# First layer of a two-layer kernel: weight split in halves, an earlier input split, and two gate products moved to where dummy transposes stood

## The reference

```
x = x + attn0(layernorm(x))      # gated, scanned linear attention, 6 heads of 64
x = x + moe(layernorm(x))        # router over 16 experts (top 2), plus 2 shared experts
x = x + attn1(layernorm(x))      # causal softmax attention, 16 heads of 128
x = x + ffn(layernorm(x))        # 688 wide, weights looked up from a table of 16 values
```

```
state = rotate(state, phi) * sigmoid(alpha) + sigmoid(beta) * rotate(v, psi)
out   = rotate(state, -theta)
y     = (out * rms(out) * rms_w * silu(g)) @ Wo
```

## Time and profile before

| | us |
|---|---|
| median of 3 runs | 2258.48 (2257.07 to 2265.22) |
| the profiled execution, its own time | 2264.6 |
| its span, first to last instruction | 2262.8 |
| first layer up to the expert pass, about | 515 |
| PE busy in the span | 2157.7 (95%) |
| DVE busy | 1678.0 (74%) |
| ACT busy | 1375.8 (61%) |
| POOL busy | 539.8 (24%) |
| mean granted clock of TensorE | 0.979 |

### The profile page before, as it was taken

The page is one execution under the profiler, slowest core; times in us unless marked ns, Lnnn a source line. Parts: engine busy times, 40 slices in busy tenths (PEclk is TensorE's granted clock), DMA queues, the critical chain, the costliest instruction groups (busy, mean ns, idle before and its releaser), DMA issues. The chain is left out here.

```text
span 2262.8 us, 37592 instructions
## 1 busy us (share of the span) xinstructions
PE 2157.7 (95%) x13012; PEld 1869.8 (83%) x13012; DVE 1678.0 (74%) x4385; ACT 1375.8 (61%) x3554; POOL 539.8 (24%) x522
## 2 busy tenths in 40 slices
PE   6899999878998999999999999999999999999995
PEld 5677777746788899889988988998898898899884
DVE  7888897788875777876776776686677678767663
ACT  4543443025646766775786777578667767856861
POOL 0212322420113323222311312222232132122210
PEclk9999999888999999999999999999999999999998
DMA  8001000326641112111211211211121121111100
GB/s 290 1 1 52 24 33 24 129 97 197 177 126 38 61 52 66 57 43 61 71 38 38 89 43 38 80 52 38 61 71 50 40 75 57 38 52 52 40 4 19
DMA packets 88539, 145.81 MB, mean 64 GB/s; under 512 B 8352, under 2 KB 55840, under 8 KB 88352
## 3 DMA queue, kind: packets, MB, share of 16 engines
q1 hardware_dynamic: 67104, 111.94, 15.5%
q0 software_dynamic: 6144, 16.79, 2.1%
q10 hardware_dynamic: 15104, 14.68, 1.9%
HBM read 105.63 MB, written 37.75 MB: 63 GB/s over the span
## 5 line engine op out<-in xcount | busy, mean ns | idle before, releaser
L585 POOL TENSOR_TENSOR wo_low<-wraw_o,wo_high 128x256 fp32r<-128x256 f32 x128 | 94.5, 739 | 1101.3 <-ACT wo_high L630 1101.3
L922 ACT ACTIVATE pr<-bank,negmax 128x128 f32<-128x128 f32 (+3 forms) x512 | 263.1, 527 | 143.5 <-DVE negmax L1447 143.5
L1037 DVE TENSOR_TENSOR p_low<-bank,p_high 128x512 fp32r<-128x512 f32 (+2 forms) x384 | 190.1, 550 | 116.2 <-ACT p_high L630 115.8
L630 ACT ACTIVATE p_high<-bank 128x512 fp32r<-128x512 f32 (+2 forms) x384 | 177.8, 497 | 150.0 <-PE bank L1946 150.0
L1447 DVE CUSTOM_DVE_ANT_0 bank<-bank,causal 128x128 f32<-128x128 f32 (+3 forms) x512 | 234.6, 520 | 1.1 <-PE bank L1602 1.1
L1474 DVE SCALAR_TENSOR_TENSOR xs<-bank,rinv,xs 128x256 f32<-128x256 f32 x512 | 211.6, 474 | 1.2 <-PE bank L1602 1.2
L1600 PE MATMUL bank<-h_high,wqk_high 128*128 128x512 f32 x512 | 203.1, 397 | 2.2 <-DVE h_low L1037 2.2
L1601 PE MATMUL bank<-h_low,wqk_high 128*128 128x512 f32 x512 | 203.1, 397 | 0.0
L1602 PE MATMUL bank<-h_high,wqk_low 128*128 128x512 f32 x512 | 202.7, 396 | 0.0
L575 POOL TENSOR_TENSOR wqk_low<-wraw,wqk_high 128x512 fp32r<-128x512 f32 x128 | 165.6, 1294 | 82.8 <-ACT wqk_high L630 82.8
L1037 DVE TENSOR_TENSOR z_low<-bank,z_high 128x512 fp32r<-128x512 f32 x128 | 88.4, 691 | 129.0 <-ACT z_high L630 128.9
(11 more groups left out here) (312 smaller groups left out, 6457.4 us busy)
## 6 DMA issues: line engine op xcount, KB each, us to landing
wraw<-in_wpair SPq DMA_DIRECT2D x64, 512.0 KB, 4.0
wraw<-in_wpair SPq DMA_DIRECT2D x64, 256.0 KB, 4.4
wraw_o<-in_wpair SPq DMA_DIRECT2D x64, 256.0 KB, 2.5
tokens_by_expert<-zero SPq DMA_DIRECT2D x10, 1024.0 KB, 10.5
xt<-tokens_by_expert SPq DMA_DIRECT2D x40, 256.0 KB, 3.2
expert_results<-ey ACTq DMA_DIRECT2D x40, 256.0 KB, 3.7
wres<-in_wexp SPq DMA_DIRECT2D x1, 6144.0 KB, 20.6
xs<-x_between_stages SPq DMA_DIRECT2D x8, 512.0 KB, 4.5
```

Source lines behind the costliest of these rows:

```text
L585: pool.tensor_tensor(wo2[e][1][:], wraw_o[r][:, e, :], wo2[e][0][:].bitcast(F32), ALU.subtract).then_inc(s_wo, 1)
L630: sc.activation(dst, src, ACT.Copy, scale=scale).then_inc(done, 1)
L922: ins = sc.activation(pr[:, i, 0:(i + 1) * P], score(i), ACT.Exp, scale=-1.0, bias=negmax[:, i:i + 1], accum_out=rsum[:, i:i + 1])
L1037: v.tensor_tensor(at(parts[1]), src, high_, ALU.subtract).then_inc(done, 1)
```

## The change

- ACT runs a one-column Copy into a new tile `warm` before anything else.
- The high part of the weights is made in two instructions instead of one: quantities 0 to 3 as soon as the loads are in, then unit 0's normalisation (unit_apply), then the wait for POOL's copies and quantities 4 to 7. DVE's low part is made in two halves too, with input_low(0) between them. PE waits for the second half before the first gate products.
- ACT does input_high(1) after gates(0, (8, 9)), ahead of sin_cos(0, 2) and gates(0, (10, 11)).
- In the loop the gate products of places 10 and 11 go from behind places 8 and 9 to behind conv_products(y, 2), where the 44 dummy transposes stood, which go away. ACT reads these two products after router_norm(x) and scales them after router_input(x). The second half of the router's transposes waits for that reading. Semaphore counts follow.

```diff
-MIDDLE_TURNS = (12, 44)
+MIDDLE_TURNS = 12
@@ ACT
+            sc.activation(warm[:], ident[:, 0:1], ACT.Copy)
...
-            sc.wait_ge(s_setup, 2)
-            high(w8[0] ... all eight quantities, s_w8h)
-            unit_apply(0, 0, xu[0], xn1, s_xn1, s_ln1)
+            sc.wait_ge(s_const, 16 * CONST_DMAS)
+            high(w8[0][:, :, 0:4, :] ..., s_w8h)
+            unit_apply(0, 0, xu[0], xn1, s_xn1, s_ln1)
+            sc.wait_ge(s_setup, 2)
+            high(w8[0][:, :, 4:8, :] ..., s_w8h)
             input_high(0)
...
             gates(0, (8, 9))
+            input_high(1)
             sin_cos(0, 2)
             gates(0, (10, 11))
-            input_high(1)
...
                 spread_rms(x)
-                gates(y, (10, 11))
                 sin_cos(y, 0)
...
                 router_norm(x)
+                gates_taken(y, (10, 11))
                 router_input(x)
+                gates_scaled(y, (10, 11))
                 sin_cos(y, 2)
@@ DVE
-            v.wait_ge(s_w8h, 1)
-            v.tensor_tensor(w8[1][:], w8raw[:], w8[0][:].bitcast(F32), ALU.subtract).then_inc(s_w8l, 1)
-            input_low(0)
+            for n in range(2):
+                quants = slice(4 * n, 4 * n + 4)
+                v.wait_ge(s_w8h, n + 1)
+                v.tensor_tensor(w8[1][:, :, quants, :], ..., ALU.subtract).then_inc(s_w8l, 1)
+                if n == 0:
+                    input_low(0)
@@ PE, gate_products
-                    if p >= 2:
+                    if p >= 10 and u > 0:
+                        pe.wait_ge(s_res, 2 * u)
+                    elif p >= 2:
                         pe.wait_ge(s_gr, 12 * u + p - 1)
+                    elif u == 1:
+                        pe.wait_ge(s_gr, 12)
@@ PE, loop
             conv_products(0, 0, (2, 3))
+            pe.wait_ge(s_w8l, 2)
             gate_products(0, (0, 1, 2, 3))
...
-                gate_products(y, (8, 9, 10, 11))
+                gate_products(y, (8, 9))
...
                 conv_products(y, 2, (2, 3))
-                pe.wait_ge(s_res, 2 * x + 1)
-                clock_turns(MIDDLE_TURNS[1], 6)
-                router_turn(x)
+                gate_products(y, (10, 11))
+                unit_turn(x, xm, s_xm, (6, 7, 4, 5), s_t2, (0,))
+                pe.wait_ge(s_gr, 12 * y + 12)
+                unit_turn(x, xm, s_xm, (6, 7, 4, 5), s_t2, (1,))
```

More of the change, by code:

```diff
@@ L162, in two_layer_program @@
             half_pi = sa("half_pi", [P, 1])
+            warm = sa("warm", [P, 1])
             headsum = sa("headsum", [P, 4])
@@ L679, in gates, with gates_taken @@
             def gates(u, places):
+                gates_taken(u, places)
+                gates_scaled(u, places)
+            def gates_taken(u, places):
                 for p in places:
@@ L691, in gates, with gates_scaled @@
                         sc.activation(dst, src, ACT.Tanh, scale=0.5).then_inc(s_gr, 1)
+            def gates_scaled(u, places):
                 for p in places:
@@ L749, in shared_silu @@
                 sc.activation(sg2[n % 2][:], bank[shared_bank(u, n)][:], ACT.Silu).then_inc(s_ss, 1)
+            sc.wait_ge(s_const, 16 * CONST_DMAS)
+            high(w8[0][:, :, 0:4, :].rearrange("p k q n -> p k (q n)"),
+                 w8raw[:, :, 0:4, :].rearrange("p k q n -> p k (q n)"), s_w8h)
+            unit_apply(0, 0, xu[0], xn1, s_xn1, s_ln1)
             sc.wait_ge(s_setup, 2)
-            high(w8[0][:].rearrange("p k q n -> p (k q n)"), w8raw[:].rearrange("p k q n -> p (k q n)"), s_w8h)
-            unit_apply(0, 0, xu[0], xn1, s_xn1, s_ln1)
+            high(w8[0][:, :, 4:8, :].rearrange("p k q n -> p k (q n)"),
+                 w8raw[:, :, 4:8, :].rearrange("p k q n -> p k (q n)"), s_w8h)
             input_high(0)
@@ L1286, in _ @@
             v.wait_ge(s_const, 16 * CONST_DMAS)
-            v.wait_ge(s_w8h, 1)
-            v.tensor_tensor(w8[1][:], w8raw[:], w8[0][:].bitcast(F32), ALU.subtract).then_inc(s_w8l, 1)
-            input_low(0)
+            for n in range(2):
+                quants = slice(4 * n, 4 * n + 4)
+                v.wait_ge(s_w8h, n + 1)
+                v.tensor_tensor(w8[1][:, :, quants, :], w8raw[:, :, quants, :], w8[0][:, :, quants, :].bitcast(F32),
+                                ALU.subtract).then_inc(s_w8l, 1)
+                if n == 0:
+                    input_low(0)
             v.wait_ge(s_const2, 16 * CONST2_DMAS)
@@ L1659, in rms_turn @@
                 if r == 2 and u + 1 < NU:
-                    pe.wait_ge(s_gr, 12 * (u + 1) + 11)
+                    pe.wait_ge(s_gr, 12 * (u + 1) + 9)
                 for i in range(NT):
@@ L1669, in out_product @@
                 if ab == 1 and u + 1 < NU:
-                    pe.wait_ge(s_gr, 12 * (u + 1) + 12)
+                    pe.wait_ge(s_gr, 12 * (u + 1) + 10)
                 half = slice(ab * P // 2, (ab + 1) * P // 2)
@@ L1702, in out_product_part @@
                     ins.then_inc(s_o0, 1)
-            def router_turn(u):
-                pe.wait_ge(s_res, 2 * u + 2)
-                unit_turn(u, xm, s_xm, (6, 7, 4, 5), s_t2)
             def router_logits_part(u, ab):
@@ L1795, in _ @@
                 gate_products(y, (4, 5))
-                clock_turns(MIDDLE_TURNS[0], 7)
+                clock_turns(MIDDLE_TURNS, 7)
                 square_sums(x, 1)
```

## The result

The changed kernel takes 2271.06 us (median of 12 runs, 2267.35 to 2276.68) against 2257.43 for the kernel before on the same chip: ratio 1.0061, 95% interval 1.0049 to 1.0072, so 13.6 us slower. The forecast was 2264 us, within 0.5% as the likeliest case and slower by over 0.5% with a chance of 0.20. The time lies in the range of 2249 to 2277; the first comparison lies just on the slow side of 0.5%, the second just within.

What follows compares the result with a forecast made beforehand. PE, busy 95% of the span, was taken as the bound through its waits and half-clock time in the first layer. -8.0 + 4.5 + 9.5 = +6 on the median of 2258.5 gave 2264 us, range 2249 to 2277.

Steps and rivals of the forecast that it cites:

- The start and the first boundary: Start and step from unit 0 to unit 1: rexp of y = 1 earlier, -8.0 us, bounds -5.3 and -10.5.
- the 5 us: Sign at the step from unit 0 to unit 1: the forecast is wrong if that boundary gives less than 5 us.
- The lead of the input itself: Unit 1's input: with input_high(1) first, DVE's low part ends 5.3 us earlier, the start's 0.7 included.
- POOL beside DVE: Unit 1's first rotation: POOL's two beta multiplications slow DVE, cost 1.1 us, at least 0, up to 2.2.
- PE is ahead of DVE there: Unit 1 after the early input: PE has no half clock and no wait of 4.9; gate products 8 and 9 end at 103.5.
- The rms turns: Three loop turns: removing products 10 and 11 gains 0, leaves PE idle 3.1 us; clock falls cost 1.5 each, +4.5 us.
- The router's part: Three turns: gate reading delays hm and logits by 1.1 us, clock falls before the logits; +9.5 us, bounds 1.1 and 6.2 each.
- The 0.8 taken off: Router's ranks: they end their wait for PE and ACT within 0.4 of each other at two turns, so 0.8 us less.
- The first (the clock does not care): Rival: neither new gap, before the rms turns or at the router, makes the clock fall; -4.7 us, 2254 us, chance 0.22.
- the second (transposes are as good as idle): Rival: router costs only 1.1 us each, the gap at the rms turns is real; -0.2 us, 2258 us, chance 0.12.
- The third: Rival: double-length falls before the rms turns, +10.2 us, and later rise at the router, +14.6; 2275 us, chance 0.16.
- The fourth: Rival: first boundary pays fully and more, the fall at 101 vanishes, no falls; -10.5 - 1.7, 2246 us, chance 0.07.

Runs made afterwards that it cites:

- e9: The changed kernel measured once more, with no further edit: 2272.31 us against 2260.80 for the kernel before, ratio 1.0039.
- e2: The kernel before with only the loop's change (gate products 10 and 11 moved, no 44 dummy transposes): 2269.17 us, ratio 1.0050.
- e10: e1 without the 44 dummy transposes, gates 10 and 11 at their old place: ratio to the kernel before 1.0002.
- e3: The changed kernel with 20 dummy transposes between gate product 11 and the transposes of xm: ratio to the kernel before 1.0023.
- e1: The kernel before with only the new start (warm, weights in halves) and the earlier input_high(1), loop unchanged: 2254.24 us, ratio 0.9981.
- e4: The changed kernel with 24 dummy transposes between gate product 9 and the rms turns: ratio to the kernel before 1.0026.
- e8: The changed kernel with rexp between gates 8 and 9, gates 10 and 11 read before router_norm, 20 dummy transposes before xm's: 2252.09 us, ratio 0.9954.
- e5: The changed kernel with gates 10 and 11 read by ACT before router_norm instead of between xm and hm: ratio to the kernel before 1.0013.

## Why the prediction was right, and where it was not

**The start and the first boundary: the term that was mis-sized.** The forecast was -8.0 us at the rms turns of y = 1; the first profile shows -4.3, outside the bounds of -5.3 to -10.5 and under the 5 us that the prediction named as a sign of being wrong. e9, the same kernel with the early rise of the clock, has its rms turns at 108.52, so -6.1, within the bounds. Either is short of -8.0. The lead of the input itself came as worked out (4.7 for 5.3). Two steps behind it failed. POOL beside DVE cost 2.1 us, where I took 1.1 and had 2.2 as the bound: the two DVE instructions that meet POOL's two are each about 1 us longer, and that half of the rotation is over by then did not help, since the rest still met both. And that PE is ahead of DVE there, with no half clock and no long wait, was wrong. PE runs into a wait of 2.70 us for ge, which stands on ACT behind the tap values, and these behind the first scan; then the clock falls from 81.8 to 85.2. The old fall between 73.7 and 80.5 is replaced by a new one. All kernels with the early input have it, 3.4 us long and starting between 79.9 and 82.4. From 81.4 on PE sets the pace: ACT waits 2.17 us for gate product 9, which ends at 107.2, not at 103.5. One thing helped without being counted in the -8.0: the fall that the kernel before had from 101.0 to 104.4 is gone. It is gone in e2 as well, whose code up to there is that of before but for products 10 and 11, and whose rms turns come at 113.82, so 0.8 of the 4.3 us need nothing of the change.

**The rms turns: right in what they wait for, lucky in the size.** Taking the products out there brought nothing forward: from the first shared_down to the next rms turns it is 43.80 us at y = 2, where it was 43.76. The gap is 3.1 us as worked out. A fall costs 2.7, between the 1.7 and 3.4 of the forecast. 1.5 us a turn were put down; over the 18 turns with the gap open it is nine long falls at 2.7 and three short ones at 1.6, so 29.1 / 18 = 1.6. The 1.5 came from expecting a short fall in nearly every turn; what came was mostly a long one or none, and that the mean agrees is luck. In the changed kernel itself it was 2.7 us in all in the first profile and 8.4 in e9, for +4.5.

**The router's part: right but for one term.** +9.5 were forecast; xm to ranks grew by 3.5, 3.2 and 3.2 us, +9.9, by 10.9 in e9, and by 3.1 in each turn of e2. The pieces hold: the second eight transposes start 2.9 us after the first at y = 1, where it was 1.9 (+1.0 for a forecast of +1.1), 1.97 us for 1.09 at half clock, and logits of 7.01, where 7.1 was worked out from the rows of two turns. e10 gives the clock's part by itself, 2.7 to 2.9 a turn. The 0.8 taken off had a wrong reason: the ranks do not wait in either kernel. What came back lies in the shared products before them, which were put down as unchanged: at y = 1 they take 9.08 us for 9.73, and from the end of the logits to the ranks it is 0.65 and 0.43 us less in the first two turns and 0.17 more in the third. What the prediction did not weigh is that the new reading on ACT opens a second gap for the clock, beside delaying hm: in e3's profile the fall came ahead of the logits with the first gap nearly closed.

The rule of the Trainium skill weighed there (TensorE: Matmul & The Clock Gate, Part 4: PE-mode transpose), that transposes do not count as activity as matmuls do, would have made e10 the equal of e1. The runs disagree for this kernel: without the 44 transposes the logits take 7.00 for e1's 5.62 us at y = 1 and xm to ranks 2.7 us more.

**The sum.** -4.3 + 3 x 1.6 + 9.9 = 10.4 us, where the forecast had 6.0; 3.7 of the 4.4 between them are the first boundary. The medians gave 13.6 and 11.5, the ratios 13.8 and 8.8. With the first profile's own falls the sum is -4.3 + 2.7 + 9.9 = 8.3, with e9's -6.1 + 8.4 + 10.9 = 13.2; so one execution and the next differ by more than what is left over, and it is not traced to a place. e9's interval of the ratio holds 10.4 (1.0046), while that of the first comparison starts just above it (1.0049).

**The rivals.** The first (the clock does not care) and the second (transposes are as good as idle) are refuted by e4 and e10. The third had the right side and half of the reason: long falls behind the rms turns did come, in one turn of the first profile and in all three of e9, 2.7 us each rather than 3.4, while the +14.6 at the router did not come (9.9 and 10.9). The fourth is refuted by the first boundary, though the fall at 101 did vanish.

**The two profiled executions.** Their spans differ by 4.6 us, the units' ends by more: the first shared_down of unit 2 starts at 400.02 before and 407.97 after. The rest, to the end of the first layer at expert_row, took 107.0 us before and 103.7 after. The windows of that last part, in the kernel before and then in e1:

```profile
400.00:507.00 107.00, 92.04 (x452) 69.78 (x452) 83.01 (x205) 16.72 (x27) 39.60 (x37) 0.84 0.30 113
```

```profile
397.00:494.00 97.00, 80.50 (x452) 62.93 (x452) 82.92 (x206) 16.61 (x27) 40.78 (x37) 0.95 0.33 124
```

The same 452 matmul records at a clock of 0.84 and 0.95. Over the fourteen profiles the last part took from 97.0 (e1) to 111.5 us (e8), though none of the changes touches its code, and 107.0 in before is among the long ones. Single profiles of this kernel are good for spans inside the loop and not for totals.

## What to carry to other kernels

Before moving work into a place that only keeps an engine busy, ask what the work was covering at its old place; here it covered PE's wait for ACT's rexp, so the move bought nothing and opened a gap there. Then look at who must read the result at the new place: put the reading where its engine is waiting anyway, not between two steps of the path. The gain that the move was capable of lay in the wait that remained: running rexp in ACT's idle time made it real, and with the gaps closed and the start of e1 the kernel became 0.46% faster than before.

## What the runs showed that was not expected

- In the one profiled execution of each: a gap of 1.83 us on PE between two groups of eight transposes, with 0.21 us before them and 0.69 behind, was followed by a fall of the clock before the logits in all three turns of e3; the gap of 2.65 us before sixteen transposes without a pause between them in e5 was too.
- A gap of 3.1 us before the rms turns was followed by a fall in 12 of 18 turns; the changed kernel itself had one in 1 of 3 turns in one execution and in 3 of 3 in another, so the same code at the same place has either level.
- With the same start, the clock rose at 18.0 to 19.0 us in five executions and at 23.2 to 24.4 in the others, and in the kernels with the early input unit 1's low part came some 1.7 us earlier with the early rise.
- A DVE scan of 128x512 beside a POOL multiplication took 2.19 us instead of 1.22.
